# Weighing four steps and multiplying seven steps behind the scores in a two-layer graph-attention kernel

## The chip, the cores and the metric

One core of one Trainium2 chip. The metric is the device time of one execution in microseconds; three runs of the kernel before gave 1599.6, 1600.88 and 1602.52 us, median 1600.88.

## The reference

x is 4096 x 256, adj is 4096 x 4096, W has two layers of 256 x 512, all float32.

```python
def _gat_layer(x, W, adj):
    proj = x @ W
    Wh, Ws = jnp.split(proj, 2, axis=-1)
    scores = Wh @ Ws.T
    a = jax.nn.softmax(scores, axis=-1) * adj
    out = a @ Wh
    out = out + x
    return jax.nn.leaky_relu(out, NEG_SLOPE)      # NEG_SLOPE = 0.01
...
y = x
for l in range(2):
    y = _gat_layer(y, W_stack[l], adj)
return _layernorm(x + y)
```

## The kernel before

Every float32 product is made of three (or, with the transposed attention, two) products of a high and a low part of type float32r: the high part is a rounded copy made by ScalarE, the low part is the difference, made by VectorE or GpSimd.

**Tiles, chunks, steps.** The 4096 rows of a layer are 32 tiles of 128 rows; each tile's scores are four chunks of 128 x 1024 (CHUNKS = 128 a layer). The kernel is software pipelined over steps, one chunk a step, and each engine runs its own instruction list, tied to the others by semaphores. A step i of the loop holds:

- TensorE: `scores(i)` (12 matmuls, L521 to L523), in some steps a "side" (a q pair for two coming tiles, made in every eighth step, with n % 8 == 6, or wh at a layer's start), then `product_of_chunk(i - LAG_PRODUCT)` (16 matmuls, L634 and L636, into one of two accumulators per tile).
- VectorE: `weigh_and_turn(i - LAG_WEIGH)` (L958 multiplies the exponentials with the row's weight and adj in place, L963 transposes 32 x 32 blocks), at a tile's boundary `row_weights(t)` (L942, L945, L947, L949: from the tile's four factors and sums the four weights), in the next step `finish_rows` (L971 to L975), in the second layer one step later `row_stats` (L987 to L994) and one later `normalise_rows` (L999), and last `chunk_max(i)` (L930, with L935 for the whole row after a tile's fourth chunk).
- ScalarE: `split_a(2k)` (the high part of half a chunk, L785), `chunk_factors(t)` at a boundary (L772), `split_a(2k + 1)`, its share of the block moves, then `exponentials(i)` (L764), which needs the maximum of the same step.
- GpSimd: the two low parts of the chunk (`split_a`, L1128), then the load of the adj chunk two ahead (L330).
- SP: the block moves (`move_blocks`, L348, 64 KB each, 5 to 7 of the 8 of a chunk; ScalarE's queue takes the others), stores and loads of rows.

The exponentials of a chunk lie in a ring of seven slots (RING = 7): `exponentials(i)` waits until chunk i - 7 was moved out. Moved blocks go to a place for two chunks (a unit) in `turned`. `scores(i)` waits for `exponentials(i - 2)`, since the scores' PSUM is double buffered. A low part is made from a high part that is made after the exponentials of the step before; the product takes it behind the scores of its own step.

**Closings.** The last four steps of each layer and what is left behind them are written out by hand on each engine: `last_steps`, `close_first` (which also transposes and splits the next layer's x, L729 and L894) and `close_second`. There `place_of` puts the high and low parts of the last chunks into space of x_t that is free, `LOW_BY_DVE` names the low parts that VectorE makes (`low_a`, L894) and GpSimd makes the others, and GpSimd's waits `pool.wait_ge(a_done, ...)` stand only ahead of loads.

The order on VectorE within a step is this (L1093 to L1098, and L1112):

```python
if weighed_at(step) is not None:
    weigh_and_turn(weighed_at(step))
if ready is not None:
    row_weights(ready)
if done is not None:
    finish_rows(done)
...
chunk_max(chunk_at(step))
```

## Time and profile before

| | |
|---|---|
| median of three runs | 1600.88 us |
| the profiled execution | 1602.16 us |
| its span, first to last instruction | 1600.4 us |
| TensorE busy (matmul) | 1556.9 us, 97% |
| VectorE busy | 1349.2 us, 84% |
| ScalarE busy | 646.9 us, 40% |
| GpSimd busy | 800.8 us, 50% |
| mean granted TensorE clock | 0.994 |

The profile is one execution. A group or timeline row gives an instruction's line in the kernel, its engine, what it writes and reads, its duration and, in square brackets, how long its engine stood idle before it and who released it. Busy time of matmuls overlaps, since they are pipelined, so a single matmul's duration is more than its share of the time; starts are the better measure. In the 40 slices of the page TensorE is at nine tenths or more in all but the first, one in the first closing and the last.

### The profile page before, as it was taken

To read this page: it belongs to the slowest core of one execution; us is meant where nothing else is said; L and a number is where in the kernel's file an instruction comes from. 1 tells how busy PE (TensorE), PEld (TensorE's weight loads), DVE (VectorE), ACT (ScalarE), POOL (GpSimd) and SP (SyncE) were. 2 spreads that over 40 slices of the span, in tenths; PEclk is the share of its full clock that TensorE was granted. 3 is DMA by queue.
4 is the path that set the end of the run, shared out by engine and by line. 5 is a ranking of instruction groups with operands and counts; after the bars stand their busy time and mean duration, and the time that the engine had idled before them with its cause. 6 is when DMAs were issued, how large, how long until landed. Compare 5 with 4: busy or idle time off the path is not lost.

```text
span 1600.4 us, 23327 instructions
## 1 busy us (share of the span) xinstructions
PE 1556.9 (97%) x8104; PEld 1320.4 (83%) x8104; DVE 1349.2 (84%) x1569; ACT 646.9 (40%) x1175; POOL 800.8 (50%) x801
## 2 busy tenths in 40 slices
PE   6999999999999999999899999999999999999996
PEld 6888888888888888888787888888888888888875
DVE  4688778877887788788847899999999999999988
ACT  4344444344444444443434444443344444444432
POOL 0055555555555555555422555555555555555554
PEclk9999999999999999999899999999999999999999
DMA  5277767676777777678924777787777777777784
GB/s 190 75 189 192 198 184 201 185 202 188 199 191 197 195 192 200 190 200 210 240 92 120 197 194 211 191 202 189 206 197 205 197 207 198 194 208 195 203 221 119
DMA packets 166981, 302.57 MB, mean 189 GB/s; under 512 B 39760, under 2 KB 67408, under 8 KB 166736
## 3 DMA queue, kind: packets, MB, share of 16 engines
q1 hardware_dynamic: 104896, 131.97, 32.6%
q0 software_dynamic: 37200, 135.28, 29.6%
q10 hardware_dynamic: 24768, 33.85, 7.8%
q8 instruction: 63, 1.03, 0.3%
q14 instruction: 54, 0.44, 0.1%
HBM read 157.29 MB, written 9.44 MB: 104 GB/s over the span
## 4 chain that ended last, share of the span: by engine, by line
PE 88%; DVE 6%; DMA 2%; issue 1%; SPq 1%; ACT 1%; POOL 1%; ACTq 0%; POOLq 0%
PE banks L634 27%; PE banks L521 16%; PE banks L523 15%; PE banks L522 15%; PE banks L636 14%; DVE ring L958 2%; SPq L348 1%; DVE ring L963 1%; DVE x_t L894 1%; DVE neg_max L930 1%; DMA turned<-ring 1%; POOL a_lo L1128 1%; DMA ring<-x_scratch 0%; PE banks L564 0%; ACT ring L764 0%
## 5 line engine op out<-in xcount | busy, mean ns | idle before, releaser
L1128 POOL TENSOR_TENSOR a_lo<-turned,a_hi 128x512 fp32r<-128x512 f32 x488 | 627.4, 1301 | 626.1 <-ACT a_hi L785 624.2
L634 PE MATMUL banks<-wh,a_hi 128*128 128x512 f32 x1952 | 700.0, 398 | 7.1 <-POOL a_lo L1128 6.9
L764 ACT ACTIVATE ring<-banks,neg_max 128x1024 f32<-128x1024 f32 x256 | 286.1, 1118 | 850.0 <-DVE neg_max L930 839.0
L636 PE MATMUL banks<-wh,a_lo 128*128 128x256 f32 x1952 | 548.8, 281 | 0.0
L930 DVE TENSOR_REDUCE neg_max<-banks 128x1 f32<-128x1024 f32 x256 | 311.9, 1219 | 166.8 <-PE banks L523 166.8
L634 PEld LDWEIGHTS banks<-wh,a_hi 128*128 128x128 f32 x1952 | 367.8, 188 | 96.9 <-POOL a_lo L1128 7.1
L521 PE MATMUL banks<-x_t,q_t 128*128 128x512 f32 x1024 | 407.7, 398 | 6.8 <-DVE q_t L894 6.8
L523 PE MATMUL banks<-x_t,q_t 128*128 128x512 f32 x1024 | 402.9, 393 | 0.0
L522 PE MATMUL banks<-x_t,q_t 128*128 128x512 f32 x1024 | 401.0, 392 | 0.0
L636 PEld LDWEIGHTS banks<-wh,a_lo 128*128 128x128 f32 x1952 | 369.4, 189 | 7.9
L958 DVE SCALAR_TENSOR_TENSOR ring<-ring,weight,load 128x1024 f32<-128x1024 f32 x254 | 328.4, 1293 | 0.8 <-DMA load<-adj 0.7
L963 DVE STREAM_TRANSPOSE ring<-ring 128x1024 f32<-128x1024 f32 x256 | 318.9, 1246 | 8.8
L785 ACT ACTIVATE a_hi<-turned 128x512 fp32r<-128x512 f32 x488 | 288.6, 623 | 31.3 <-PE banks L636 28.1
L521 PEld LDWEIGHTS banks<-x_t,q_t 128*128 128x128 f32 x1024 | 192.8, 188 | 51.4 <-DVE q_t L894 6.0
L523 PEld LDWEIGHTS banks<-x_t,q_t 128*128 128x128 f32 x1024 | 192.6, 188 | 48.0
L522 PEld LDWEIGHTS banks<-x_t,q_t 128*128 128x128 f32 x1024 | 193.4, 189 | 34.1
L330 POOL DMA_DIRECT2D load<-adj x254 | 145.7, 574 | 145.4 <-DVE ring L958 119.8
L975 DVE SCALAR_TENSOR_TENSOR rows<-rows 128x256 f32<-128x256 f32 x62 | 81.7, 1318 | 2.1
L949 DVE TENSOR_SCALAR weight<-factor,row_inv 128x4 f32<-128x4 f32 x64 | 52.5, 820 | 2.2
L764 ACT ACTIVATION_READ_ACCUMULATOR ring<-banks,neg_max 128x1 f32 x256 | 48.6, 190 | 0.0
L634 PE MATMUL banks<-wh,x_t 128*128 128x512 f32 x96 | 37.0, 423 | 11.4 <-DVE x_t L894 6.9
L894 DVE TENSOR_TENSOR wh<-banks,wh 128x512 fp32r<-128x512 f32 x32 | 21.2, 688 | 26.2 <-ACT wh L745 26.2
(81 smaller groups left out, 895.7 us busy)
## 6 DMA issues: line engine op xcount, KB each, us to landing
load<-adj POOLq DMA_DIRECT2D x254, 512.0 KB, 5.1
turned<-ring SPq DMA_DIRECT2D x1504, 64.0 KB, 4.0
turned<-ring ACTq DMA_DIRECT2D x496, 64.0 KB, 3.2
ring<-x SPq DMA_DIRECT2D x8, 512.0 KB, 5.8
rows<-x SPq DMA_DIRECT2D x32, 128.0 KB, 3.4
x_scratch<-rows SPq DMA_DIRECT2D x32, 128.0 KB, 2.9
rows<-x_scratch SPq DMA_DIRECT2D x30, 128.0 KB, 3.5
first_rows<-x SPq DMA_DIRECT2D x30, 128.0 KB, 3.1
```

The costliest lines, as they stand in the source:

```text
L330: queue.dma_start(adj_at(i), adj_chunks[n // CPT, n % CPT]).then_inc(adj_loaded[adj_buffer[i]], 16)
L521: nc.tensor.matmul(out_ap, s_hi, m_hi, start=j == 0, stop=False)
L522: nc.tensor.matmul(out_ap, s_hi, m_lo, start=False, stop=False)
L523: last = nc.tensor.matmul(out_ap, s_lo, m_hi, start=False, stop=j == len(operands) - 1)
L634: nc.tensor.matmul(psum[:, bank, :], of_hi[:, b], wh[:, k].rearrange("p a d -> p (a d)"), start=start, stop=stop, skip_group_check=True)
L636: last = nc.tensor.matmul(psum[:, bank, 0:D], of_lo[:, b], wh[:, k, 0], start=False, stop=stop, skip_group_check=True)
L764: nc.scalar.activation(ring_at(i).rearrange("p (r b j) -> p b r j", r=2, j=QUAD), psum[:, 2 * (i % 2):2 * (i % 2) + 2, :].rearrange("p h ( ...
L785: nc.scalar.activation(operand(0, j).rearrange("p b (r j) -> p b r j", r=QUADS), as_f32(turned_in[unit_place(unit)][:, :, b:b + SUB, :]).r ...
L930: nc.vector.tensor_reduce(neg_max[:, of:of + 1], psum[:, 2 * (i % 2):2 * (i % 2) + 2, :].rearrange("p b e -> p (b e)"), AXIS_X, ALU.max, n ...
L958: nc.vector.scalar_tensor_tensor(ring_at(i), ring_at(i), weight[:, of:of + 1], adj_at(i), ALU.mult, ALU.mult).then_inc(a_done, 1)
L963: nc.vector.transpose(ring_at(i), ring_at(i)).then_inc(blocks_turned, 1)
L1128: nc.gpsimd.tensor_tensor(operand(1, j).rearrange("p b (r j) -> p b r j", r=QUADS), as_f32(turned_in[unit_place(unit)][:, :, b:b + SUB, :] ...
```

## The change

The diff does four things.

1. LAG_WEIGH goes from 5 to 4 and LAG_PRODUCT from 8 to 7; the ring keeps its seven slots.
2. In the loop on VectorE `row_weights` stands ahead of `weigh_and_turn`.
3. The closings are rewritten for seven chunks behind the last scores: the orders on every engine, the places, and which low parts VectorE makes. `row_weights` of the last tile follows the last maximum at once, and ScalarE makes the last exponentials and factors ahead of two high parts.
4. In the closings GpSimd waits for a weighing (`a_done`) ahead of single subtractions, and VectorE's own low parts stand between a weigh and its turn.

```diff
@@ -35,8 +35,8 @@
     GROUPS = N // GROUP
     PAIRS = TILES // 2
     WPAIRS = TILES // 2
-    LAG_WEIGH = 5
-    LAG_PRODUCT = 8
+    LAG_WEIGH = 4
+    LAG_PRODUCT = 7
     LAG_ROWS = 13
 
     LAST_STEPS = CHUNKS - 4
@@ -228,7 +228,7 @@
 
         def place_of(j):
             of_layer, m = divmod(j, SUBS)
-            if m >= 2 * CLOSED and (m < 2 * CLOSED + 8 or of_layer == LAYERS - 1):
+            if m >= 2 * CLOSED and (m < 2 * CLOSED + 6 or of_layer == LAYERS - 1):
                 return 2 + m - 2 * CLOSED
             return m % 2
 
@@ -242,7 +242,7 @@
             return x_t[:, part, kt, start:start + BANK].rearrange("p (b e) -> p b e", e=P)
 
 
-        LOW_BY_DVE = [(0, 1, 3), tuple(range(1, 16, 2))]
+        LOW_BY_DVE = [(0, 1, 3, 5), (0, 1, 3, 5, 7, 9, 11, 13)]
         low_made, low_counts, user_before, last_user = {}, [0, 0], {}, {}
         for j in range(LAYERS * SUBS):
             by_dve = j % SUBS - 2 * CLOSED in LOW_BY_DVE[j // SUBS]
...
@@ -665,20 +665,19 @@
                 last_steps(CHUNKS)
                 transpose_x(8)
                 product_of_chunk(CLOSED)
+                transpose_x(9)
                 product_of_chunk(CLOSED + 1)
-                transpose_x(9)
-                product_of_chunk(CLOSED + 2)
                 transpose_x(10)
                 transpose_x(11)
+                product_of_chunk(CLOSED + 2)
+                transpose_x(12)
                 product_of_chunk(CLOSED + 3)
-                transpose_x(12)
-                product_of_chunk(CLOSED + 4)
                 transpose_x(13)
                 transpose_x(14)
+                product_of_chunk(CLOSED + 4)
                 product_of_chunk(CLOSED + 5)
+                make_side(("q", PAIRS))
                 product_of_chunk(CLOSED + 6)
-                make_side(("q", PAIRS))
-                product_of_chunk(CLOSED + 7)
 
             def close_second():
                 last_steps(2 * CHUNKS)
...
@@ -805,46 +804,44 @@
                 split_a(j - 8)
                 chunk_factors(last - 1)
                 split_a(j - 7)
+                move_blocks(end - 8)
                 exponentials(end - 4)
                 split_a(j - 6)
                 split_a(j - 5)
-                move_blocks(end - 8)
+                move_blocks(end - 7)
                 exponentials(end - 3)
                 split_a(j - 4)
                 split_a(j - 3)
-                move_blocks(end - 7)
                 exponentials(end - 2)
                 split_a(j - 2)
                 split_a(j - 1)
                 move_blocks(end - 5)
+                exponentials(end - 1)
+                chunk_factors(last)
                 split_a(j)
                 split_a(j + 1)
-                exponentials(end - 1)
-                chunk_factors(last)
-                split_a(j + 2)
-                split_a(j + 3)
 
             def close_first():
                 j = 2 * CLOSED
                 last_steps(CHUNKS, j, TILES - 1)
                 split_x(8)
-                for n in (4, 5, 6, 7):
+                for n in (2, 3, 4, 5):
                     split_a(j + n)
                 move_blocks(CHUNKS - 4)
                 move_blocks(CHUNKS - 3)
                 split_x(9)
                 move_blocks(CHUNKS - 2)
-                split_a(j + 8)
-                split_a(j + 9)
+                split_a(j + 6)
+                split_a(j + 7)
                 move_blocks(CHUNKS - 1)
                 split_x(10)
                 split_x(11)
-                split_a(j + 10)
+                split_a(j + 8)
                 split_x(12)
-                split_a(j + 11)
+                split_a(j + 9)
                 split_x(13)
                 split_x(14)
-                for n in (12, 13, 14, 15):
+                for n in (10, 11, 12, 13):
                     split_a(j + n)
                 split_side(("q", PAIRS))
 
...
@@ -1019,30 +1016,33 @@
                 weigh(i)
                 turn_blocks(i)
 
-            def last_steps(end, last):
-                weigh_and_turn(end - 9)
+            def last_steps(end, j, last):
                 row_weights(last - 1)
+                weigh_and_turn(end - 8)
                 chunk_max(end - 4)
-                weigh_and_turn(end - 8)
                 weigh_and_turn(end - 7)
                 chunk_max(end - 3)
                 weigh_and_turn(end - 6)
                 chunk_max(end - 2)
+                weigh_and_turn(end - 5)
+                finish_rows(last - 3)
+                chunk_max(end - 1)
+                row_weights(last)
+                low_a(j)
+                weigh(end - 4)
+                low_a(j + 1)
+                turn_blocks(end - 4)
+                weigh(end - 3)
+                low_a(j + 3)
+                turn_blocks(end - 3)
 
             def close_first():
                 j = 2 * CLOSED
-                last_steps(CHUNKS, TILES - 1)
-                finish_rows(TILES - 4)
-                weigh_and_turn(CHUNKS - 5)
-                chunk_max(CHUNKS - 1)
-                low_a(j)
-                low_a(j + 1)
-                row_weights(TILES - 1)
-                weigh_and_turn(CHUNKS - 4)
-                low_a(j + 3)
-                weigh_and_turn(CHUNKS - 3)
+                last_steps(CHUNKS, j, TILES - 1)
                 split_x(8)
-                weigh_and_turn(CHUNKS - 2)
+                weigh(CHUNKS - 2)
+                low_a(j + 5)
+                turn_blocks(CHUNKS - 2)
                 weigh_and_turn(CHUNKS - 1)
                 finish_rows(TILES - 3)
                 for g in (9, 10, 11, 12, 13):
@@ -1054,28 +1054,20 @@
 
             def close_second():
                 j, end, last = SUBS + 2 * CLOSED, LAYERS * CHUNKS, LAYERS * TILES - 1
-                last_steps(end, last)
-                weigh_and_turn(end - 5)
-                finish_rows(last - 3)
-                chunk_max(end - 1)
-                low_a(j + 1)
-                row_weights(last)
-                weigh_and_turn(end - 4)
-                low_a(j + 3)
-                weigh_and_turn(end - 3)
+                last_steps(end, j, last)
+                weigh(end - 2)
                 low_a(j + 5)
-                weigh_and_turn(end - 2)
-                low_a(j + 7)
+                turn_blocks(end - 2)
                 weigh_and_turn(end - 1)
                 finish_rows(last - 2)
+                low_a(j + 7)
+                row_stats(last - 3)
                 low_a(j + 9)
-                row_stats(last - 3)
-                low_a(j + 11)
                 normalise_rows(last - 3)
                 finish_rows(last - 1)
                 row_stats(last - 2)
+                low_a(j + 11)
                 low_a(j + 13)
-                low_a(j + 15)
                 normalise_rows(last - 2)
                 row_stats(last - 1)
                 normalise_rows(last - 1)
@@ -1090,10 +1082,10 @@
                     continue
                 ready, done, of_stats, whole = (tile_at(step - CPT), finish_at.get(step), stats_at.get(step),
                                                 normalise_at.get(step))
+                if ready is not None:
+                    row_weights(ready)
                 if weighed_at(step) is not None:
                     weigh_and_turn(weighed_at(step))
-                if ready is not None:
-                    row_weights(ready)
                 if done is not None:
                     finish_rows(done)
                 if whole is not None:
@@ -1150,19 +1142,18 @@
                 load_group(nc.gpsimd, g)
 
             def last_steps(end, j):
-                load_next_adj(end - 9)
                 split_a(j - 8)
                 split_a(j - 7)
                 load_next_adj(end - 8)
                 split_a(j - 6)
                 split_a(j - 5)
                 load_next_adj(end - 7)
-                load_next_adj(end - 6)
                 split_a(j - 4)
                 split_a(j - 3)
+                load_next_adj(end - 6)
                 split_a(j - 2)
+                split_a(j - 1)
                 load_next_adj(end - 5)
-                split_a(j - 1)
 
                 wait_moved(pool, end - 7)
                 load_adj(nc.gpsimd, end - 2)
@@ -1175,16 +1166,19 @@
             def close_first():
                 j, end = 2 * CLOSED, CHUNKS
                 last_steps(end, j)
-                split_a(j + 2)
                 load_next_x(10)
                 load_last_adj(end)
-                for n in range(4, 12):
+                for n in (2, 4):
+
+                    pool.wait_ge(a_done, end - 4 + n // 2)
                     split_a(j + n)
-
                 pool.wait_ge(a_done, end)
+                for n in (6, 7, 8, 9):
+                    split_a(j + n)
+
                 for i in range(2):
                     load_adj(nc.gpsimd, end + i)
-                for n in range(12, 16):
+                for n in range(10, 14):
                     split_a(j + n)
 
             def load_late_rows():
@@ -1196,17 +1190,18 @@
             def close_second():
                 j, end, last = SUBS + 2 * CLOSED, LAYERS * CHUNKS, LAYERS * TILES - 1
                 last_steps(end, j)
-                split_a(j)
-                split_a(j + 2)
                 load_last_adj(end)
-                split_a(j + 4)
+                for n in (2, 4):
+
+                    pool.wait_ge(a_done, end - 4 + n // 2)
+                    split_a(j + n)
+                load_late_rows()
+                pool.wait_ge(a_done, end)
                 split_a(j + 6)
-                load_late_rows()
                 split_a(j + 8)
+                invert_std(last - 3)
                 split_a(j + 10)
-                invert_std(last - 3)
                 split_a(j + 12)
-                split_a(j + 14)
                 for t in range(last - 2, last + 1):
                     invert_std(t)
 
```

## Rows read from the trace of the kernel before

**Rows 1.** Busy by stretch: us, then PE, PEld, DVE, ACT, POOL, PEclk, DMA, GB/s.

```profile
100.00:700.00 600.00, 600.00 (x3069) 507.24 (x3068) 487.07 (x532) 246.15 (x455) 318.85 (x312) 1.00 0.72 194
900.00:1500.00 600.00, 600.00 (x3068) 507.21 (x3067) 564.74 (x690) 246.14 (x455) 339.77 (x338) 1.00 0.75 200
```

**Rows 2.** Timeline of VectorE, boundary of a second-layer tile: start us, duration us, instruction.

```profile
1210.30 1.23 DVE L930 TENSOR_REDUCE neg_max<-banks 128x1 f32<-128x1024 f32 x1 [0.73 <-PE banks L523]
...
1211.63 1.27 DVE L958 SCALAR_TENSOR_TENSOR ring<-ring,weight,load 128x1024 f32<-128x1024 f32 x1
...
1214.11 0.57 DVE L942 TENSOR_TENSOR scaled_sum<-factor,chunk_sum 128x4 f32<-128x4 f32 x1
...
1215.11 0.83 DVE L949 TENSOR_SCALAR weight<-factor,row_inv 128x4 f32<-128x4 f32 x1
...
1215.89 1.23 DVE L930 TENSOR_REDUCE neg_max<-banks 128x1 f32<-128x1024 f32 x1
```

**Rows 3.** Timeline of ScalarE in the same tile: a high part and the factors.

```profile
1212.66 0.62 ACT L785 ACTIVATE a_hi<-turned 128x512 fp32r<-128x512 f32 x1
...
1213.19 0.28 ACT L772 ACTIVATE factor<-neg_max,row_neg_max 128x4 f32<-128x4 f32 x1
```

**Rows 4.** Timeline of GpSimd in the same tile: its two subtractions, merged.

```profile
1213.37 2.54 POOL L1128 TENSOR_TENSOR a_lo<-turned,a_hi 128x512 fp32r<-128x512 f32 x2 [2.11 <-ACT a_hi L785]
```

**Rows 5.** Timeline of TensorE: the first product matmul behind the next scores.

```profile
1215.69 0.39 PE L634 MATMUL banks<-wh,a_hi 128*128 128x512 f32 x1
```

**Rows 6.** Timeline of VectorE, the other maxima around that tile.

```profile
1205.07 1.21 DVE L930 TENSOR_REDUCE neg_max<-banks 128x1 f32<-128x1024 f32 x1
...
1221.72 1.21 DVE L930 TENSOR_REDUCE neg_max<-banks 128x1 f32<-128x1024 f32 x1
...
1227.44 1.21 DVE L930 TENSOR_REDUCE neg_max<-banks 128x1 f32<-128x1024 f32 x1
...
1234.08 1.22 DVE L930 TENSOR_REDUCE neg_max<-banks 128x1 f32<-128x1024 f32 x1 [1.07 <-PE banks L523]
```

**Rows 7.** Timeline of VectorE, maxima of the first layer.

```profile
399.37 1.23 DVE L930 TENSOR_REDUCE neg_max<-banks 128x1 f32<-128x1024 f32 x1 [2.73 <-PE banks L523]
...
421.75 1.22 DVE L930 TENSOR_REDUCE neg_max<-banks 128x1 f32<-128x1024 f32 x1 [1.90 <-PE banks L523]
...
438.53 1.23 DVE L930 TENSOR_REDUCE neg_max<-banks 128x1 f32<-128x1024 f32 x1 [1.68 <-PE banks L523]
```

**Rows 8.** Timeline of VectorE and GpSimd, row weights at start and in the first closing.

```profile
57.73 0.15 DVE L942 TENSOR_TENSOR scaled_sum<-factor,chunk_sum 128x4 f32<-128x4 f32 x1
...
58.30 0.23 DVE L949 TENSOR_SCALAR weight<-factor,row_inv 128x4 f32<-128x4 f32 x1
...
749.16 2.53 POOL L1128 TENSOR_TENSOR a_lo<-turned,a_hi 128x512 fp32r<-128x512 f32 x2 [0.74 <-ACT a_hi L785]
...
749.29 1.18 DVE L942 TENSOR_TENSOR scaled_sum<-factor,chunk_sum 128x4 f32<-128x4 f32 x1 [0.42 <-ACT factor L772]
...
750.89 0.83 DVE L949 TENSOR_SCALAR weight<-factor,row_inv 128x4 f32<-128x4 f32 x1
```

**Rows 9.** Timeline of GpSimd, VectorE and TensorE, first closing.

```profile
778.46 4.95 POOL L1128 TENSOR_TENSOR x_t<-turned,x_t 128x512 fp32r<-128x512 f32 x4
...
778.82 5.15 DVE L894 TENSOR_TENSOR x_t<-w_part,x_t 128x512 fp32r<-128x512 f32 x1
...
784.01 0.80 PE L634 MATMUL banks<-wh,x_t 128*128 128x512 f32 x1 [4.49 <-DVE x_t L894]
```

**Rows 10.** Timeline of GpSimd and VectorE, second closing.

```profile
1536.98 2.55 POOL L1128 TENSOR_TENSOR a_lo<-turned,a_hi 128x512 fp32r<-128x512 f32 x2
...
1537.34 2.22 DVE L942 TENSOR_TENSOR scaled_sum<-factor,chunk_sum 128x4 f32<-128x4 f32 x1
```

**Rows 11.** TensorE wait, second closing; stretch of the first (busy, PEclk, DMA, GB/s).

```profile
1552.80 0.50 PE L634 MATMUL banks<-wh,a_hi 128*128 128x512 f32 x1 [2.16 <-POOL a_lo L1128]
...
784.00:786.00 2.00, 1.99 (x6) 0.50 1.04 188
```

More of the change, by code:

```diff
@@ L336, in sp_moves @@
             layer, n = divmod(i, CHUNKS)
-            last = [8, 5, 5, 8, 5, 6, 5, 6, 6] if layer == 0 else [8, 5, 5, 8, 5, 5, 4, 4, 4]
+            last = [5, 5, 8, 5, 6, 5, 6, 6] if layer == 0 else [5, 5, 8, 5, 5, 4, 4, 4]
             count = last[n - CHUNKS + len(last)] if n >= CHUNKS - len(last) else 5 if i % 2 else 7
@@ L459, in close_first @@
             def close_first():
-                for i in range(CHUNKS - 9, CHUNKS - 4):
+                for i in range(CHUNKS - 8, CHUNKS - 4):
                     move_blocks(i)
@@ L484, in close_second @@
                 store_rows(last - 4)
-                for i in range(end - 9, end - 6):
+                for i in range(end - 8, end - 6):
                     move_blocks(i)
@@ L722, in split_x @@
                 if g == GROUPS + 4:
[L724 removed]
+                    act.wait_ge(product_done, 2 * CLOSED + 6)
                 if g == GROUPS:
@@ L854, in close_second @@
                 move_blocks(end - 4)
+                split_a(j + 2)
+                split_a(j + 3)
+                move_blocks(end - 3)
                 split_a(j + 4)
                 split_a(j + 5)
-                move_blocks(end - 3)
+                move_blocks(end - 2)
                 split_a(j + 6)
                 split_a(j + 7)
-                move_blocks(end - 2)
-                split_a(j + 8)
-                split_a(j + 9)
                 move_blocks(end - 1)
-                for n in range(10, 16):
+                for n in range(8, 14):
                     split_a(j + n)
```

1 line of the change is left out of this document (removed).

## The prediction

> **What bounds the kernel now.** I read the stretches first: in 100 to 700 us (first layer) and in 900 to 1500 us (second layer) TensorE is busy for all 600 of 600 us at a granted clock of 1.00, while VectorE is busy 487 and 565 us [rows 1]. So in the steady loops nobody else has any time to give, and the only thing an edit there can do is to break TensorE's cover. Idle time of TensorE exists only in the start and the two closings; the largest single wait stands in [rows 9].
>
> Next I read one tile of the loop, engine by engine. A tile is four steps; I call T the start of the maximum of its last chunk (1210.30 in the second layer). VectorE then weighs and turns the *previous* tile's last chunk (2.48 us from the start of L958 to that of L942), then makes the row weights (L942 to L949), then takes the next maximum at 1215.89 = T+5.59 [rows 2]. ScalarE meanwhile does the exponential, one high part, and only then the four factors, which end at 1213.47 = T+3.17 [rows 3]. GpSimd's two subtractions run from T+3.07, 1.27 us each, to T+5.61 [rows 4]. TensorE starts the next step's product at 1215.69 = T+5.39 [rows 5]; the low part that this product needs was ready at T+3.07+1.27 = T+4.34, plus 0.1 for the semaphore. That gives the slack that decides everything: 5.39 - 4.44 = **0.95 us**. A maximum that starts more than 0.95 us behind its scores delays exponential, high part, low part, and then TensorE.
>
> **The change, part by part.** *Lags of 4 and 7.* Weighing and product both move one step earlier, so the three steps between them stay. Each exponential waits for the moves of the chunk seven before, which were issued two steps earlier and now three: a wait gets looser, but it ended last nowhere, so it gives nothing. SP, ACT and GpSimd issue the same transfers per step. The chunk that SP moves on a tile's boundary is now the even one. None of this costs anything as long as four steps stay the cover of a transfer's landing.
>
> *Row weights ahead of the weighing.* With a lag of 4 the first chunk of a tile is weighed in the step in which its row weights are made, so the order on VectorE is turned round: row weights, weigh, turn, maximum. Before, the weigh and turn of the chunk before (2.48 us) covered the wait for the factors. Now nothing does. VectorE is free at about T+1.4 and stands until T+3.2, when the factors are there: **1.8 us idle**, and queued behind that wait are the weigh, the turn and the next maximum.
>
> When does the block of row weights end? L942 took 0.57 and L949 0.83 us in this tile, but 0.15 and 0.23 us at the start of the kernel, when GpSimd does nothing [rows 2, 8]. In the loop L942 ends at 1214.68 and L949 at 1215.94, just behind the ends of GpSimd's two subtractions (1214.64 and 1215.91) [rows 2, 4]. They wait for GpSimd, so starting them earlier doesn't end them earlier. The trace even has the case: in the closing L942 starts at 749.29, 0.13 us after GpSimd, ends at 750.47 at GpSimd's first end, and L949 then again stands until the second [rows 8]. So row weights still end at T+5.64. The weigh and turn come behind: 5.67 + 2.48 = T+8.15 for the next maximum, against T+5.59 on time. It is 2.56 us late, 2.56 - 0.95 = **1.61 us of TensorE idle** in the next step.
>
> This is also where a rule of the Trainium skill speaks against the change: GPSIMD Engine Reference, Key points, says that GpSimd shares its SBUF interfaces with VectorE and contends with VectorE instructions in a 2-port mode or with two SBUF inputs. L942 has two such inputs; the trace agrees by its 0.57 against 0.15 us. Without that rule the sum would be that of the fourth case below.
>
> The delay then runs on. From one maximum to the next VectorE needs 5.83 us in the following step (1215.89 to 1221.72), 5.72 to 5.74 in the one with the row statistics of the second layer, and 4.50 (1205.07 to 1210.30 less its 0.73 idle) or, with a q side, 5.57 (1227.44 to 1234.08 less 1.07) in the last [rows 2, 6]. A step of TensorE takes 5.59, the period of a tile is 22.38, and 23.78 with a q side in it, which is every second tile [rows 6, 7].
> - First layer: product of step 1 at T+8.15+4.44 = 12.59. Step 2 is due at 18.18; its low part comes from the maximum at 13.98, so at 18.42, another 0.24 idle. In step 2 VectorE has 1.68 us of idle in the trace [rows 7] and has caught up. Sum 1.61 + 0.24 = 1.85 without a q side; with one, its matmuls hide the 0.24: 1.6. Mean 1.72.
> - Second layer: the statistics leave no such idle. Maxima at 8.15, 13.98, 19.72; the last at 24.23 by VectorE, while TensorE, which idles 0.15 more in step 3, gives 24.36: a period of 24.36 against 22.38, +1.98. With a q side 25.37 against 23.78, +1.59. Mean 1.79.
>
> In each layer tiles 1 to 29 have this boundary in the loop with products behind it (tile 0 falls in the start, 30 and 31 in the closing): 29 x 1.72 + 29 x 1.79 = **+101.8 us**.
>
> *Closings.* Seven chunks are left behind the last scores instead of eight; TensorE's total is unchanged. The gain is in GpSimd's order: four subtractions in a row shut VectorE's low part out, which took 5.15 us, and TensorE waited 4.49 us for it and ran at half clock behind [rows 9, 11]. With subtractions let go one at a time, each behind a weighing, most of that goes; what is late next is the weigh, turn and move chain behind the last scores, which has one chunk's product (2.8 us) less to cover it, and the row weights there now stand bare as well. I take -4 for both closings and the start together, with +4 and -12 as bounds.
>
> Sum: the profiled execution is 1602.2 us (span 1600.4 and 1.8 around it). 1602.2 + 101.8 - 4 = 1700; it lies 1.3 above the median of the runs, so in terms of the median **1698 us**.
>
> **The clock.** A new stall of 1.6 us in every tile might cost the clock as well. The trace has idle of 2.16 us with a stretch of half clock behind, and 4.49 us the same, with 0.50 granted in 784 to 786 us, the level of 1.2 GHz [rows 9, 11]. Both are longer than 1.6, so I charge nothing, and keep it for the upper bound.
>
> **Rivals.** (1) *GpSimd shuts the row weights out for both subtractions.* In the closing L942 stood 2.22 us, until two back-to-back subtractions were both done [rows 10]. Then L945 to L949 (0.6 us) and the weigh end 0.65 us later: 58 x 0.65 = +38, 1736 us, and a 2.2 us stall that could touch the clock. Against it: there both high parts were ready before VectorE asked; in the loop the factors sit between them, as in the 749 us case. (2) *VectorE gets in between.* L942 slips ahead of the first subtraction, L949 behind it, the weigh ahead of the second: next maximum near T+7.05, stalls of about 0.5 + 0.24 and some 0.4 less where a q side hides them. About 0.63 a tile, 58 x 0.63 = +37, with the closings' -4: 1634 us. (3) *Row weights free of GpSimd, and the closings gain all: faster.* If both small operations took their 0.15 and 0.23 us, row weights would need about 0.9: 3.2 + 0.9 + 2.5 = T+6.6, 1.0 late against a slack of 0.95. That is the point from which it decides: below T+6.54 there is no stall. The loops cost 0.2 a tile, +12; the closings would give back their stalls behind collisions (4.49, 2.16 and a like one in the first closing [rows 9, 11], and about 2.5 and twice 1.7 lost at half clock behind them, estimated from the starts of the matmuls there: 14.7) and some 7 us of the shorter stalls behind them. 1602.2 + 12 - 22 - 1.3 = 1591 us. Against it are all the rows where small operations stand for GpSimd. (4) *It does nothing that shows*: as (3) in the loops with the closings at -12: 1601 us.
>
> **How the numbers follow.** Forecast 0.70 (1675 to 1720), rival 1 0.09, rival 2 0.10, rival 3 0.06, rival 4 0.05. The range must leave out no more than 0.2: I let out rivals 3 and 4 and a little of the rest, 1625 to 1740. About 0.2% (3 us) is what a measurement of this kernel can tell from no change. Slower by more: 0.70 + 0.09 + 0.10 = 0.89; same 0.05; faster 0.06.
>
> **What would show it.** In the changed kernel: L942 with idle of about 1.8 us before it, released by ScalarE's factor, in some 60 places; L942 lengthened to some 1.1 us and L949 still near 0.8; on TensorE about 58 waits of 1.6 us for GpSimd's low part in the step behind each boundary, and TensorE's busy share down from 97% to about 92%; the period of a tile near 24.2 to 24.4 us without a q side and 25.4 with one; a granted clock of 1.00 in the loops. VectorE's idle before its maxima should be gone in the second layer. In the first closing no low part of 5 us. It is wrong if L942 finds its factors ready, if the weigh starts well before T+5.6, or if the low part still meets the product.

## The result, and the profile after

The changed kernel took **1712.7 us** (median of four runs, 1711.4 to 1713.7) against 1601.7 of the kernel before in runs beside it: 1.069 times, 95% interval 1.067 to 1.071. The forecast of 1698 with a range of 1625 to 1740 holds, 15 us low. The profiled execution has a span of 1710.4 us against 1600.4, so 110.0 us are to be placed. Beside the experiments the kernel before was run again and took 1595 to 1609 us, but for one slow run of 6375.6 us that is left out everywhere.

All lines behind the diff moved: the maximum is L927 now, the row weights L939 to L946, weigh L955, turn L960, the high part L784, the factors L771, GpSimd's subtraction L1120, VectorE's low part L891. TensorE's lines are the same.

The page of the changed kernel, its engines and three of its costliest groups (busy and mean ns of one, then idle time and what ended it):

```profile
PE 1583.3 (93%) x8104; PEld 1316.0 (77%) x8104; DVE 1377.7 (81%) x1570; ACT 644.9 (38%) x1175; POOL 803.4 (47%) x800
...
L634 PE MATMUL banks<-wh,a_hi 128*128 128x512 f32 x1968 | 721.3, 406 | 90.9 <-POOL a_lo L1120 90.9
...
L939 DVE TENSOR_TENSOR scaled_sum<-factor,chunk_sum 128x4 f32<-128x4 f32 x64 | 71.5, 1117 | 112.4 <-ACT factor L771 112.4
...
L946 DVE TENSOR_SCALAR weight<-factor,row_inv 128x4 f32<-128x4 f32 x64 | 50.5, 789 | 2.2
```

Both waits that the prediction named are there and are the largest of their engines. The view of the waits, its two rows for them (total, times, longest):

```profile
PE banks L634 <- POOL a_lo L1120: 90.9, 64, 5.7
...
DVE scaled_sum L939 <- ACT factor L771: 112.4, 62, 3.2
```

The windows of the steady loops, which answer to [rows 1]: TensorE is busy 567 of 600 us where it was busy for all 600, and the granted clock stays at its upper level (the 0.99 comes from a wait of 3.41 us at 920 us, which still belongs to the start of the second layer).

```profile
100.00:700.00 600.00, 567.19 (x2858) 469.72 (x2857) 469.14 (x495) 229.50 (x424) 295.96 (x290) 1.00 0.66 180
900.00:1500.00 600.00, 566.91 (x2850) 467.93 (x2849) 530.65 (x625) 226.43 (x421) 308.16 (x307) 0.99 0.68 183
```

One boundary of a tile in the first layer, from the timeline of the changed kernel with T = 402.83 (start, duration, engine; idle before it in brackets). It answers to [rows 2 to 5]:

```profile
402.83 1.23 DVE L927 TENSOR_REDUCE neg_max<-banks 128x1 f32<-128x1024 f32 x1 [2.10 <-PE banks L523]
...
405.72 0.29 ACT L771 ACTIVATE factor<-neg_max,row_neg_max 128x4 f32<-128x4 f32 x1
405.90 2.54 POOL L1120 TENSOR_TENSOR a_lo<-turned,a_hi 128x512 fp32r<-128x512 f32 x2 [2.17 <-ACT a_hi L784]
...
406.04 1.18 DVE L939 TENSOR_TENSOR scaled_sum<-factor,chunk_sum 128x4 f32<-128x4 f32 x1 [1.79 <-ACT factor L771]
...
407.64 0.83 DVE L946 TENSOR_SCALAR weight<-factor,row_inv 128x4 f32<-128x4 f32 x1
...
408.51 1.29 DVE L955 SCALAR_TENSOR_TENSOR ring<-ring,weight,load 128x1024 f32<-128x1024 f32 x1
...
411.00 1.18 DVE L927 TENSOR_REDUCE neg_max<-banks 128x1 f32<-128x1024 f32 x1
...
414.03 2.50 POOL L1120 TENSOR_TENSOR a_lo<-turned,a_hi 128x512 fp32r<-128x512 f32 x2 [3.37 <-ACT a_hi L784]
...
415.35 0.50 PE L634 MATMUL banks<-wh,a_hi 128*128 128x512 f32 x1 [1.36 <-POOL a_lo L1120]
```

VectorE stands 1.79 us for the factors; L939 takes 1.18 us and ends 0.05 us behind GpSimd's first subtraction (405.90 + 1.27 = 407.17); L946 ends at 408.47, behind the second (408.44). The next maximum starts at T+8.17 instead of T+5.59, and TensorE stands for the low part that comes of it. The last row starts at T+12.52.

The 110.0 us by the starts of the maxima in both traces, counted from 0:

| stretch | before | after | difference |
|---|---|---|---|
| start to maximum 11 | 98.5 | 105.1 | +6.6 |
| first layer, maxima 11 to 123 (28 tiles) | 646.5 | 694.5 | +48.1, 1.72 a tile |
| first closing, 123 to 128 | 71.6 | 69.9 | -1.7 |
| start of the second layer, 128 to 139 | 70.5 | 76.2 | +5.7 |
| second layer, 139 to 251 (28 tiles) | 646.5 | 694.8 | +48.3, 1.73 a tile |
| second closing, 251 to the end | 66.9 | 69.9 | +3.0 |

The two loop rows are firm: the 646.5 us came out again to 0.1 us in the profile of the experiment *waits in the first closing* below, which is the kernel before with one edit in its first closing. The other four rows are not. In that profile, though its start and second closing are the kernel before's code, the start takes 103.3 us instead of 98.5 and the second closing 64.1 instead of 66.9; the start of the second layer agrees (71.1).

### The profile page after: what moved, and what is told of

Its sections match the earlier page's. It is cut to its first block, busy times and chain, and to the rows that moved or that the text cites. A ratio compares the mean times of both kernels' runs of the same rounds, so it can differ in the third digit from the quotient of the medians.

```text
span 1710.4 us, 23333 instructions
## 1 busy us (share of the span) xinstructions
PE 1583.3 (93%) x8104; PEld 1316.0 (77%) x8104; DVE 1377.7 (81%) x1570; ACT 644.9 (38%) x1175; POOL 803.4 (47%) x800
## 4 chain that ended last, share of the span: by engine, by line
PE 47%; DVE 29%; ACT 10%; issue 6%; POOL 5%; ACTq 1%; DMA 1%; SPq 1%; POOLq 0%
PE banks L634 15%; DVE neg_max L927 8%; PE banks L521 8%; PE banks L523 8%; PE banks L522 8%; PE banks L636 7%; ACT ring L763 5%; DVE ring L955 5%; DVE ring L960 5%; POOL a_lo L1120 5%; DVE scaled_sum L939 4%; ACT a_hi L784 4%; DVE weight L946 3%; ACTq L348 1%; SPq L348 1%
## 5 line engine op out<-in xcount | busy, mean ns | idle before, releaser
L1120 POOL TENSOR_TENSOR a_lo<-turned,a_hi 128x512 fp32r<-128x512 f32 x488 | 626.5, 1298 | 644.8 <-ACT a_hi L784 644.6
L634 PE MATMUL banks<-wh,a_hi 128*128 128x512 f32 x1968 | 721.3, 406 | 90.9 <-POOL a_lo L1120 90.9
L636 PE MATMUL banks<-wh,a_lo 128*128 128x256 f32 x1968 | 555.0, 282 | 0.0
L634 PEld LDWEIGHTS banks<-wh,a_hi 128*128 128x128 f32 x1968 | 372.6, 189 | 218.6 <-POOL a_lo L1120 117.7
L927 DVE TENSOR_REDUCE neg_max<-banks 128x1 f32<-128x1024 f32 x256 | 309.5, 1209 | 127.5 <-PE banks L523 126.3
L636 PEld LDWEIGHTS banks<-wh,a_lo 128*128 128x128 f32 x1968 | 374.8, 190 | 4.3
L955 DVE SCALAR_TENSOR_TENSOR ring<-ring,weight,load 128x1024 f32<-128x1024 f32 x254 | 325.5, 1282 | 2.2
L960 DVE STREAM_TRANSPOSE ring<-ring 128x1024 f32<-128x1024 f32 x256 | 318.8, 1245 | 8.6
L784 ACT ACTIVATE a_hi<-turned 128x512 fp32r<-128x512 f32 x488 | 286.7, 621 | 22.4 <-PE banks L636 16.5
L939 DVE TENSOR_TENSOR scaled_sum<-factor,chunk_sum 128x4 f32<-128x4 f32 x64 | 71.5, 1117 | 112.4 <-ACT factor L771 112.4
L946 DVE TENSOR_SCALAR weight<-factor,row_inv 128x4 f32<-128x4 f32 x64 | 50.5, 789 | 2.2
L634 PE MATMUL banks<-wh,x_t 128*128 128x512 f32 x80 | 32.9, 445 | 11.3 <-POOL x_t L1120 8.8
```

The costliest lines, as they stand in the source:

```text
L634: nc.tensor.matmul(psum[:, bank, :], of_hi[:, b], wh[:, k].rearrange("p a d -> p (a d)"), start=start, stop=stop, skip_group_check=True)
L636: last = nc.tensor.matmul(psum[:, bank, 0:D], of_lo[:, b], wh[:, k, 0], start=False, stop=stop, skip_group_check=True)
L784: nc.scalar.activation(operand(0, j).rearrange("p b (r j) -> p b r j", r=QUADS), as_f32(turned_in[unit_place(unit)][:, :, b:b + SUB, :]).r ...
L927: nc.vector.tensor_reduce(neg_max[:, of:of + 1], psum[:, 2 * (i % 2):2 * (i % 2) + 2, :].rearrange("p b e -> p (b e)"), AXIS_X, ALU.max, n ...
L955: nc.vector.scalar_tensor_tensor(ring_at(i), ring_at(i), weight[:, of:of + 1], adj_at(i), ALU.mult, ALU.mult).then_inc(a_done, 1)
L960: nc.vector.transpose(ring_at(i), ring_at(i)).then_inc(blocks_turned, 1)
```

## The experiments

My theory: at a tile's boundary the row weights wait first for ScalarE's factors and then for GpSimd's subtractions, with weigh, turn and the next maximum behind them. Rivals: only the factors' wait counts; GpSimd's length doesn't; the loss comes from lags or closings.

**Half the subtraction, the rest as changed.**

```diff
-                    operand(1, j).rearrange("p b (r j) -> p b r j", r=QUADS),
+                    operand(1, j).rearrange("p b (r j) -> p b r j", r=QUADS)[:, :half],
...
```

The two inputs are halved in the same way, and GpSimd sets its low parts to zero once at the start of the kernel.

> The changed kernel with GpSimd subtracting only the first half of each of its low parts (the other half of its low parts is left out of the computation), so its two subtractions take about 1.3 us together instead of 2.5. Theory (row weights end when GpSimd's second subtraction ends): VectorE's last row-weight operation ends near T+4.5, the next maximum starts near T+7.0, the low part is also there 0.6 us sooner, no stall of TensorE in the loops: 1612 to 1626 us. Rival (the row weights' time is their own, or the wait for the factors is all there is): next maximum still at T+8.15, 1.0 us of stall a tile, about 1665 us.

Measured, in one run: 1602.0 us, the kernel before 1603.7 beside it; I had expected 1612 to 1626. The loops cost nothing (645.6 and 645.4 us for the stretches of 646.5). The starts are still 5.8 and 4.0 us longer than before, but the closings, whose subtractions are halved too, take 64.6 and 65.8 us instead of 71.6 and 66.9. Timeline of this kernel at a boundary, T = 1119.56:

```profile
1122.44 0.29 ACT L771 ACTIVATE factor<-neg_max,row_neg_max 128x4 f32<-128x4 f32 x1
1122.63 1.44 POOL L1121 TENSOR_TENSOR a_lo<-turned,a_hi 128x256 fp32r<-128x256 f32 x2 [3.53 <-ACT a_hi L784]
...
1122.76 0.63 DVE L939 TENSOR_TENSOR scaled_sum<-factor,chunk_sum 128x4 f32<-128x4 f32 x1 [1.79 <-ACT factor L771]
...
1123.81 0.28 DVE L946 TENSOR_SCALAR weight<-factor,row_inv 128x4 f32<-128x4 f32 x1
...
1124.13 1.28 DVE L955 SCALAR_TENSOR_TENSOR ring<-ring,weight,load 128x1024 f32<-128x1024 f32 x1
```

The factors come no earlier (T+3.17) and VectorE still stands 1.79 us, but L939 and L946 shrink with the subtractions and the weigh starts at T+4.57 instead of T+5.68. So the wait for the factors alone is no loss; it becomes one with GpSimd's full subtractions behind it. The next maximum starts at 1126.62, T+7.06, and TensorE doesn't wait. That agrees with the edge that the slack gives: the low part takes 0.55 us less (1.27 less 0.72), so the slack of 0.95 grows to 1.50 and the maximum may come at T+7.09. The run doesn't divide the loss between the two effects of a shorter subtraction; it shows that both together are all of it in the loops.

**The factors ahead of the high parts.**

```diff
-                if k is not None:
-                    split_a(2 * k)
                 if summed is not None:
                     chunk_factors(summed)
                 if k is not None:
+                    split_a(2 * k)
                     split_a(2 * k + 1)
```

> The changed kernel, with the factors made on ScalarE ahead of the first high part of the step, so that they are there 0.5 us earlier, ahead of GpSimd's first subtraction. Theory (GpSimd's subtractions shut out VectorE's operations with two SBUF inputs): the small operations take 0.15 and 0.23 us, but the weigh behind them starts only behind GpSimd's first or second subtraction, so the next maximum is at T+7.1 to T+8.4 and not at T+6.1; 1655 to 1720 us. Rival (only the wait for the factors counts, and weighing is not shut out): next maximum near T+6.1, within the slack, 1612 to 1625 us.

Measured: 1707.8 us, ratio 1.065 (1.063 to 1.067), 1.64 us a tile. The timeline, T = 1117.09:

```profile
1119.77 0.16 DVE L938 TENSOR_TENSOR scaled_sum<-factor,chunk_sum 128x4 f32<-128x4 f32 x1 [1.27 <-ACT factor L771]
...
1120.35 2.54 POOL L1119 TENSOR_TENSOR a_lo<-turned,a_hi 128x512 fp32r<-128x512 f32 x2 [2.34 <-ACT a_hi L784]
1120.36 1.30 DVE L945 TENSOR_SCALAR weight<-factor,row_inv 128x4 f32<-128x4 f32 x1
...
1121.70 2.28 DVE L954 SCALAR_TENSOR_TENSOR ring<-ring,weight,load 128x1024 f32<-128x1024 f32 x1
```

Now L938 takes its 0.16 us, but the last of the four small operations meets GpSimd's start and ends with its first subtraction (1.30 us), and the weigh takes 2.28 instead of 1.28: it stands until the second is over at 1122.89 and does most of its own work behind it. The next maximum comes at T+8.09: factors half a microsecond earlier gave 0.08. Whichever operation meets the subtractions pays for them; the rival falls.

**The maximum ahead of the weighing at a boundary** (SyncE takes all moves of that chunk).

```diff
                     row_weights(ready)
+                    chunk_max(chunk_at(step))
                 if weighed_at(step) is not None:
...
-                chunk_max(chunk_at(step))
+                if ready is None:
+                    chunk_max(chunk_at(step))
```

> The changed kernel, with the maximum of a boundary step ahead of its weighing, and SP issuing all eight moves of the boundary's chunk so that ScalarE's exponentials don't wait for its turning. Theory (what VectorE loses in the wait isn't given back, and the weigh now falls into GpSimd's subtractions): the boundary's maximum is on time at T+5.65, the next one is 2.6 to 3.9 us late, 1.7 to 3 us of stall a tile in the first layer and VectorE as the bound in the second: 1690 to 1780 us. Rival (only the chain from the row weights to the maximum counts): TensorE doesn't stall in the loops, 1605 to 1625 us.

Measured: 1778.7 us, ratio 1.111 (1.107 to 1.114). The maximum is on time, 5.59 us behind the last, and the debt comes a step later, in the timeline of the next weigh:

```profile
423.21 2.54 POOL L1124 TENSOR_TENSOR a_lo<-turned,a_hi 128x512 fp32r<-128x512 f32 x2
...
423.52 3.33 DVE L957 SCALAR_TENSOR_TENSOR ring<-ring,weight,load 128x1024 f32<-128x1024 f32 x1
```

The second weigh falls on the subtractions and takes 3.33 instead of 1.27 us; the following maximum is 9.37 us behind this one. Moving the maximum alone only moves the delay, since a weigh then meets GpSimd.

**The order alone, in the kernel before (lags 5 and 8).**

```diff
-                if weighed_at(step) is not None:
-                    weigh_and_turn(weighed_at(step))
                 if ready is not None:
                     row_weights(ready)
+                if weighed_at(step) is not None:
+                    weigh_and_turn(weighed_at(step))
```

> The kernel before with one edit: in the loop on VectorE the row weights stand ahead of the weighing; lags stay 5 and 8, closings and start as before. Theory (the bare wait of the row weights for the factors, lengthened by GpSimd, is the whole loss in the loops): a tile's period of 24.2 to 24.4 us instead of 22.4, VectorE idle 1.8 us ahead of L942 in some 58 places, +96 to +102 us, so about 1697 to 1703 us. The start and the closings stay within 2 us of before. Rival (the shorter lags starve the moves and loads, and the order hardly matters): within 10 us of 1601.

Measured: 1798.4 us, ratio 1.123 (1.120 to 1.126): 3.3 us a tile, twice what I expected. So the order by itself makes a loss in the loops, with the lags left as they were. Its timeline in the step behind the boundary (T = 399.09):

```profile
407.12 1.19 DVE L930 TENSOR_REDUCE neg_max<-banks 128x1 f32<-128x1024 f32 x1
...
407.23 2.06 ACTq L348 DMA_DIRECT2D turned<-ring  x3
...
409.42 1.12 ACT L764 ACTIVATE ring<-banks,neg_max 128x1024 f32<-128x1024 f32 x1 [6.63 <-issue]
...
412.54 0.50 PE L634 MATMUL banks<-wh,a_hi 128*128 128x512 f32 x1 [2.29 <-POOL a_lo L1128]
```

and its windows behind the stall (the granted clock is the third figure from the end):

```profile
408.00:412.00 4.00, 2.24 (x10) 1.50 (x8) 3.90 (x6) 2.24 (x4) 0.77 (x1) 1.00 0.86 232
412.00:416.00 4.00, 3.46 (x13) 2.99 (x14) 3.97 (x4) 1.36 (x3) 2.43 (x3) 0.65 0.23 49
```

The maximum is 8.03 us behind T, as in the changed kernel. But with a lag of 5 the chunk moved here is an odd one, of which ScalarE issues three blocks, between the turn and the exponentials. They start 1.1 us behind the maximum's end (408.31 to 409.42), the idle of TensorE grows from 1.36 to 2.29 us, and a stretch at 0.65 of the clock follows, partly the 1.2 GHz level. In the prediction I had counted the even chunk at the boundary as worth nothing.

**The same with the blocks' parity shifted.**

```diff
-            count = ... 5 if i % 2 else 7
+            count = ... (5, 5, 7, 7)[i % 4]
```

> The order-only kernel (lags 5 and 8, row weights ahead of the weighing) again, with one more edit: SP issues seven of the eight moves of the boundary's chunk instead of five, so that ScalarE's queue has one move and not three ahead of its exponentials; another chunk takes the three. Theory (order-only lost 3.4 us a tile and not 1.7 because the three moves made the boundary's exponentials 1.0 us later, and the stall of 2.3 us that this gave took the clock down): stall back at 1.4 us, clock 1.00 in the loops, period 24.2 us, 1695 to 1705 us. Rival (the longer lags themselves make the difference between 1798 and 1713): stays above 1770 us.

Measured: 1737.2 us, ratio 1.084 (1.081 to 1.088), 2.1 to 2.2 a tile. Its timeline:

```profile
418.31 0.50 PE L634 MATMUL banks<-wh,a_hi 128*128 128x512 f32 x1 [1.23 <-POOL a_lo L1128]
...
419.58 2.21 ACTq L348 DMA_DIRECT2D turned<-ring  x3
419.71 1.21 DVE L930 TENSOR_REDUCE neg_max<-banks 128x1 f32<-128x1024 f32 x1
...
421.92 1.12 ACT L764 ACTIVATE ring<-banks,neg_max 128x1024 f32<-128x1024 f32 x1 [4.49 <-DVE neg_max L930]
```

The first stall is back at 1.23 us and the mean clock of the loops at 1.00 (0.97 and 0.96 in the order kernel), so the three issues did cause the first stall's excess; but they now stand ahead of the next step's exponentials and make a second stall (0.76 us before the product that starts at 400.10 in the period looked at). Of the 98 us between the first order kernel and 1700, 61 went with the parity. Neither side of my second expectation was met; the remaining 37 us are not split further.

**VectorE's rows in the gap.** `finish_rows` ahead of `row_weights`, with LAG_ROWS 12, so that it fills the wait for the factors.

```diff
-    LAG_ROWS = 13
+    LAG_ROWS = 12
...
+                if done is not None:
+                    finish_rows(done)
                 if ready is not None:
                     row_weights(ready)
...
```

`finish_rows` no longer stands behind the weighing, and one store of rows is no longer issued in the second closing.

> The changed kernel, with a tile's finish_rows one step earlier, ahead of the row weights, where VectorE stands idle for the factors. Theory (the chain from the last maximum over exponentials, factors, row weights, weigh and turn to the next maximum makes the stall, whatever else VectorE does): VectorE's idle ahead of the row weights shrinks from 1.8 to about 0.45 us, the stall of 1.4 us in the next step stays, only the second, small one goes: 4 to 17 us faster, 1696 to 1708 us. Rival (VectorE's total is the limit): the filled gap comes back in full in the second layer, 35 us or more faster, under 1680 us.

Measured: 1708.3 us, ratio 1.067 (1.063 to 1.070). Idle ahead of L938 falls from 1.79 to 0.53 us, and the maximum is again 8.17 behind T:

```profile
402.01 1.23 DVE L926 TENSOR_REDUCE neg_max<-banks 128x1 f32<-128x1024 f32 x1 [1.90 <-PE banks L522]
...
405.22 1.18 DVE L938 TENSOR_TENSOR scaled_sum<-factor,chunk_sum 128x4 f32<-128x4 f32 x1 [0.53 <-ACT factor L770]
...
414.53 0.50 PE L633 MATMUL banks<-wh,a_hi 128*128 128x512 f32 x1 [1.37 <-POOL a_lo L1119]
```

1.26 us of work a tile moved into idle time of VectorE gave 4.4 us in all (the loops lose 1.61 and 1.68 a tile instead of 1.72 and 1.73), since the end of the row weights is pinned. The gain lies at the low end of the expected 4 to 17 us: the theory holds and the rival falls.

**The closings.** Three kernels. First the changed one without GpSimd's waits for single weighings:

```diff
-                for n in (2, 4):
-                    pool.wait_ge(a_done, end - 4 + n // 2)
-                    split_a(j + n)
-                pool.wait_ge(a_done, end)
-                for n in (6, 7, 8, 9):
+                for n in (2, 4, 6, 7, 8, 9):
                     split_a(j + n)
...
```

The wait for the last weighing now stands only ahead of the loads, and the second closing loses its waits for weighings too.

> The changed kernel without the waits for weighings ahead of GpSimd's single subtractions in the two closings (waits ahead of loads stay). Theory (the waits keep GpSimd from shutting VectorE out): 2 to 6 us slower than the changed kernel, 1714 to 1719 us, with a VectorE operation of over 3 us in the first closing. Rival (they do nothing, other waits end last): within 1.5 us of 1712.7.

Measured: 1712.2 us, ratio 1.069 (1.066 to 1.072); closings of 68.6 and 70.9 us against 69.9 and 69.9. No operation of VectorE in them takes over 3 us. The rival holds: the waits are worth nothing that shows there. Then the kernel before with such waits in its first closing (*waits in the first closing*):

```diff
                 for n in range(4, 12):
+                    if n in (4, 6, 8):
+                        pool.wait_ge(a_done, end - 4 + n // 2)
                     split_a(j + n)
-                pool.wait_ge(a_done, end)
```

> The kernel before with one part of the change alone: in the first closing GpSimd waits for a weighing ahead of its subtractions 4, 6 and 8 of the x_t places, so that four of them no longer follow each other. Theory (the 5.15 us low part was VectorE shut out, and TensorE's 4.49 us wait and the half clock behind it came from it): 3 to 6 us faster than before, 1595 to 1598 us. Rival (the weigh and move chain is late anyway): within 1.5 us of before.

Measured: 1602.2 us against 1601.3, ratio 1.000 (0.998 to 1.002), where I had expected 3 to 6 us less. The first closing takes 70.3 us instead of 71.6, which is less than this stretch differs between the two order kernels, whose closings are the kernel before's (68.6 and 72.1). Its timeline, where [rows 9] had a low part of 5.15 us and a wait of 4.49:

```profile
784.20 0.65 DVE L894 TENSOR_TENSOR x_t<-w_part,x_t 128x512 fp32r<-128x512 f32 x1
...
793.10 1.09 PE L564 MATMUL banks<-ident,ring 128*128 128x128 f32 x8 [1.71 <-DMA ring<-x_scratch]
...
799.59 0.47 PE L634 MATMUL banks<-wh,a_hi 128*128 128x512 f32 x1 [1.74 <-POOL a_lo L1128]
...
805.29 1.09 PE L564 MATMUL banks<-ident,ring 128*128 128x128 f32 x8 [1.81 <-DMA ring<-x_scratch]
```

The collision is gone and with it the largest wait; three others, two of them for a DMA of x, end last instead. Last, the changed kernel with each chunk turned ahead of VectorE's low part:

```diff
                 weigh(end - 4)
-                low_a(j + 1)
                 turn_blocks(end - 4)
+                low_a(j + 1)
...
```

The same is done at the three other places where a low part stood between a weigh and its turn.

> The changed kernel, but in both closings each chunk is turned right behind its weighing and VectorE's low part stands behind the turn instead of between the two. My theory of the second closing: the low parts between weigh and turn hold VectorE for ScalarE's high part (2.41 and 2.87 us of idle in the changed kernel's trace), and the turn, the moves and the last products stand behind that wait. By it the second closing, 69.9 us from the last tile's first maximum to the end, becomes 2 to 5 us shorter and the execution 1707.5 to 1711 us. Rival: the moves' landing and TensorE's own work end last there anyway, and the wait only moves: within 1.5 us of 1712.7. The loops stay as they are, 8.17 us from the boundary's maximum to the next.

Measured: 1707.9 us, ratio 1.067 (1.065 to 1.069); second closing 64.8 us instead of 69.9 (before: 66.9, and 64.1 in the kernel with waits in the first closing). The four runs take 1706.8 to 1711.0 us and the changed kernel's 1711.4 to 1713.7, and the second closing takes 69.7 to 71.0 us in the four other kernels that keep VectorE's changed order there and the full subtractions. The rows of the changed kernel that this undoes, with ScalarE's queue between the two:

```profile
1679.80 2.72 ACTq L348 DMA_DIRECT2D turned<-ring  x4
1682.63 1.15 ACT L784 ACTIVATE x_t<-turned 128x512 fp32r<-128x512 f32 x2 [5.44 <-issue]
```

```profile
1683.81 1.40 DVE L891 TENSOR_TENSOR x_t<-turned,x_t 128x512 fp32r<-128x512 f32 x1 [2.87 <-ACT x_t L784]
1685.13 1.23 DVE L960 STREAM_TRANSPOSE ring<-ring 128x1024 f32<-128x1024 f32 x1
...
1691.50 0.76 PE L634 MATMUL banks<-wh,x_t 128*128 128x512 f32 x1 [3.74 <-POOL x_t L1120]
```

VectorE's low part waits for a high part that stands behind four block issues on ScalarE; the turn of a chunk already weighed stands behind it, and so do its own moves and product. In the experiment the two low parts wait 0.54 us and not at all, instead of 2.41 and 2.87. TensorE's waits there of 3.91 and 3.74 us go down to 2.2 at most, and with them the fall of the clock. The windows of the changed kernel (0.72 and 0.87) and of the experiment (1.00):

```profile
1672.00:1684.00 12.00, 7.57 (x27) 5.61 (x25) 6.72 (x7) 2.30 (x4) 2.39 (x3) 0.72 0.48 131
1684.00:1698.00 14.00, 9.54 (x45) 8.11 (x46) 12.78 (x19) 4.50 (x8) 8.82 (x10) 0.87 0.49 131
```

```profile
1672.00:1684.00 12.00, 7.92 (x41) 6.10 (x40) 11.33 (x12) 3.05 (x6) 5.04 (x7) 1.00 0.65 181
1684.00:1698.00 14.00, 11.36 (x61) 9.29 (x62) 11.97 (x27) 3.75 (x7) 7.70 (x7) 1.00 0.40 98
```

The experiment has 41 and 61 matmuls in these windows where the changed kernel has 27 and 45. This part of the change can be taken back by itself; it isn't enough against the loops' 100 us.

## Why the prediction was right, and where it was off

- **The idle of 1.8 us ahead of L942:** 62 times, 1.79 in the tile shown, as foretold.
- **Row weights pinned to both subtractions:** the heart of the forecast (T+5.64), measured T+5.64 (408.47). L939 takes 1.18 (forecast 1.1), L946 0.83 (0.8). The half subtraction, the early factors and the filled gap each show the pin from another side. The Trainium skill (GPSIMD Engine Reference, Key points) says that GpSimd contends with VectorE operations that have two SBUF inputs or run in a 2-port mode. The rows agree for L939 and the weigh, which have two inputs; L946, whose tensor input is single, is held too, and no row shows in which mode it runs.
- **Next maximum T+8.15, product T+12.59:** T+8.17 and T+12.52.
- **The loops:** forecast 1.72 a tile in the first layer, measured 1.72; in the second 1.79, measured 1.73. Periods of some 25.4 with a q side (25.38 by the sum) and 24.17 to 24.25 without one (24.23); in the second layer mostly 24.22, where I had 24.36: the last maximum comes when VectorE is free (24.23), and the 0.15 us that I had TensorE idle in the fourth step isn't there. In the loops TensorE has 56 recorded waits, one a tile, of 1.2 to 1.4 us; the 64 of the waits' view hold the starts and closings too. With the boundary of tile 1 in each start, 29 tiles a layer are about 100 us of the forecast 101.8. VectorE's idle ahead of the second layer's maxima falls from 26.3 to 4.7 us; I had said that it would be gone.
- **Rivals:** GpSimd didn't shut out L939 twice, and VectorE didn't slip in between. The faster rival's point of decision, a slack of 0.95 us less what the low part takes, agrees with the half subtractions (T+7.06 against T+7.09, no stall); no run stands just beyond it. Nothing in the change brings the kernel there. One sum of mine is off: stalls of 0.74 us, and some 0.4 less with a q side, have the mean 0.54 and not 0.63, which would put the second rival at 1628 us instead of 1634.
- **The clock:** charged nothing in the loops, and the windows give 1.00 and 0.99.
- **The step that was mis-sized** is the last term, -4 us for both closings and the start together. By the two profiled executions the starts less their boundary tile cost 4.9 and about 4.0, the closings -1.7 and +3.0: **+10** instead of -4, outside its bounds of -12 to +4. With the loops 2 us below the forecast this is the whole error of the profiled execution, 12 us; the rest of the 15 is how the two profiled executions lie to the medians. Against the profile of the kernel with waits in the first closing the two starts are 0.1 and 3.4 and the closings -0.4 and 5.8: the sum stays (9 us), its split doesn't.

Three things were wrong in that term.

First, I priced only gains for the second closing and looked at no new waits, though the diff puts low parts between weigh and turn: that is worth 5 us by the last experiment.

Second, I took a removed 4.5 us wait at nearly its price, though TensorE's next waits stood close behind. By the experiment in the kernel before, its removal gives nothing that the runs can tell.

Third, I counted the start as unchanged. There is no product ahead of step 7 there to cover VectorE, and weighing from step 4 puts a weigh and turn into a step that had none. From maximum 3 to maximum 4 the changed kernel takes 8.88 us (52.13 to 61.01) instead of 7.06 (52.17 to 59.23). The first product then waits:

```profile
80.27 0.76 PE L634 MATMUL banks<-wh,a_hi 128*128 128x512 f32 x1 [5.68 <-POOL a_lo L1120]
```

The kernel before waits twice there, 3.89 us in all. The kernel with waits in the first closing, whose start is the same code, waits twice as well, 5.69 us in all. The rows of the kernel before:

```profile
77.22 0.50 PE L521 MATMUL banks<-x_t,q_t 128*128 128x512 f32 x1 [2.57 <-DVE q_t L894]
81.55 0.47 PE L634 MATMUL banks<-wh,a_hi 128*128 128x512 f32 x1 [1.32 <-POOL a_lo L1128]
```

With the half subtractions maximum 11 is still 5.8 us late, so this part doesn't come from GpSimd's length. That 1.8 us of it is the weighing moved forward is shown by the other runs: the step from maximum 3 to 4 takes 8.88 or 8.89 us in all six kernels that weigh four steps behind and ahead of that maximum. It takes 7.06 in the four that weigh five steps behind, in whatever order, and in the one that takes the maximum ahead of the weighing. It is the same in the second layer. What makes the rest of the starts' loss is not shown.

- **Even lag:** I wrote that the parity of the moved chunk costs nothing. In the changed kernel nothing speaks against that. But the order alone, with the old lags, runs 86 us (24 with the blocks shifted) behind the changed kernel. So 61 of the 86 us hang on which chunk's issues stand at the boundary once the exponentials are late there, and I had not asked whose issues stand ahead of them. What makes the other 24 is not shown.

## What to carry to other kernels

An operation that stands until another engine's instruction ends is pinned to that end. So ask of a reordering not only how much idle it opens but which end pins the block behind it, and what covered that block before; here 2.5 us of weigh and turn lost their cover and 1.6 of them came out on the bound engine. When a lag changes, write down for every step, the starts and closings too, which chunk's DMA issues now stand ahead of which activation. A long wait removed need not give its length back: here one of 4.5 us gave nothing that shows, since others stood close behind. And a difference between two single profiles in a start or a closing is worth little until another execution of the same code agrees.

## What the runs showed of the hardware

- A small VectorE operation that met GpSimd's subtraction ended with it: the row weights' first operation takes 0.16 us alone, 0.63 beside one of 0.72 us, 1.18 beside one of 1.27. A large one ended some 1.1 us behind one subtraction, or behind two: a weigh of 1.28 us took 2.28 and 3.33.
- Granted clock and idle of TensorE: recorded idle of 1.23 to 1.37 us in every tile left it at 1.00; 2.29 us in the order kernel was followed by 0.65 in 412 to 416 us; 3.91 and 3.74 us in the second closing by the 0.72 and 0.87 above. In between the same code went both ways. In the second closing of the kernel before 2.16 us came with a clock of 0.83 in 1552 to 1562 us. In the kernel with waits in the first closing 2.17 us in the same place left 1.00 in 1556 to 1566 us, and that closing is 2.8 us shorter. The short idle costs only itself, the long one also the time at the lower clock.
- The idle that is recorded ahead of a matmul is less than the stall: 1.37 us in the kernel with the rows in the gap, where the tile's period is 1.60 to 1.64 longer (25.42 against 23.78 to 23.82) with no other recorded idle in it. Periods between starts are the better measure.
- Block issues on ScalarE's queue held back the activations behind them: in the rows shown three took 2.06 to 2.21 us, four 2.72.
